# Row sums of a correction for fractional zero points: 32 wide matmuls in place of 128 of one column, in a branch that these inputs jump over

## What is computed

```python
def xattn(x1, x2, x1_scale, x1_zp, x2_scale, x2_zp):   # fake_quant: (clip(round(x/s + z), 0, 255) - z) * s
    return matmul(fake_quant(x1, x1_scale, x1_zp), fake_quant(x2, x2_scale, x2_zp))
def ffn(x, W_base, b_base, W_router, lora_A, lora_B):   # 8 experts of rank 16, the best two per row
    w = normalised top-2 of softmax(x @ W_router.T)
    return x @ W_base.T + b_base + 2 * einsum(lora_B, lora_A @ x, w)
x = x + xattn(layernorm(x), ctx_4096)   # x: 2 x 1024 x 2048, ctx: 2 x 2048 x 2048
x = x + ffn(layernorm(x))
```

## Time and profile before

| | before |
|---|---|
| median of 3 runs | 969.04 us (966.88 to 978.15) |
| the profiled execution | 966.17 us |
| its span, first to last instruction | 964.4 us |
| TensorE busy | 906.4 us (94%) |
| VectorE, ScalarE, GpSimd busy | 610.5 us (63%), 370.9 us (38%), 146.9 us (15%) |
| DMA | 226.59 MB, mean 235 GB/s |

### The profile page before, as it was taken

The page is one execution under the profiler, slowest core; times in us unless marked ns, Lnnn a source line. Parts: engine busy times, 40 slices in busy tenths (PEclk is TensorE's granted clock), DMA queues, the critical chain, the costliest instruction groups (busy, mean ns, idle before and its releaser), DMA issues.

```text
span 964.4 us, 12403 instructions
## 1 busy us (share of the span) xinstructions
PE 906.4 (94%) x4725; PEld 432.5 (45%) x4725; DVE 610.5 (63%) x955; ACT 370.9 (38%) x337; POOL 146.9 (15%) x191
## 2 busy tenths in 40 slices
PE   0599999989999999999999999999999999999997
PEld 0244443434445455454545455444444444444443
DVE  7678578953799875546374546699655365564611
ACT  3867436754265444243324222164213323133100
POOL 2537420332100102010111100010000000000000
PEclk9999999999999999999999999999999999999999
DMA  9998999989874879999999999956479979889621
GB/s 326 346 366 292 327 323 355 305 312 357 254 226 149 226 159 274 166 252 179 241 218 223 192 259 227 364 184 227 146 167 233 228 157 244 210 182 235 150 74 44
DMA packets 269310, 226.59 MB, mean 235 GB/s; under 512 B 221632, under 2 KB 222656, under 8 KB 265280
## 3 DMA queue, kind: packets, MB, share of 16 engines
q1 hardware_dynamic: 258880, 191.15, 74.7%
q0 software_dynamic: 10368, 34.61, 10.7%
HBM read 132.29 MB, written 39.94 MB: 179 GB/s over the span
## 4 chain that ended last, share of the span: by engine, by line
PE 72%; DMA 9%; DVE 8%; issue 6%; SPq 2%; ACT 2%; POOL 1%; POOLq 0%; DVEq 0%; ACTq 0%
PE PS L1645 57%; PE PS L1577 8%; PE PS L1662 4%; PE PS L1680 4%; DMA XR<-x 2%; DMA x1d<-XR 2%; DVE XR L1089 2%; DVE ST L1012 1%; DVE ST L1096 1%; DMA Yb<-x1d 1%; DMA XV<-XU 1%; SPq L533 1%; DMA HT<-HW 1%; DMA XT<-NX 1%; POOL CU L708 1%
## 5 line engine op out<-in xcount | busy, mean ns | idle before, releaser
L1645 PE MATMUL PS<-WS,XT 128*128 128x512 f16 x2736 | 596.3, 379 | 3.5 <-DVE OQ L1343 2.2
L1645 PEld LDWEIGHTS PS<-WS,XT 128*128 128x128 f16 x2736 | 267.1, 98 | 325.9 <-DVE OQ L1343 3.7
L1577 PE MATMUL PS<-QC,QT 128*128 128x512 bf16 x1024 | 227.4, 385 | 46.0 <-ACT QT L781 37.5
L1343 DVE SCALAR_TENSOR_TENSOR OQ<-PS,ZI,OQ 128x512 f32<-128x512 f32 x124 | 90.8, 747 | 157.2 <-PE PS L1662 78.5
L1577 PEld LDWEIGHTS PS<-QC,QT 128*128 128x128 bf16 x1024 | 100.8, 99 | 171.5 <-issue 53.3
L823 ACT ACTIVATE NX<-Yb 128x1024 f16<-128x1024 f32 x52 | 54.9, 1055 | 117.2 <-DMA XT<-NX 61.3
L708 POOL TENSOR_SCALAR CU<-CS,K,S 128x1024 uint8<-128x1024 f32 x64 | 80.9, 1266 | 121.5 <-DMA CS<-ctx 103.7
L727 POOL DMA_DIRECT2D out<-OQ x64 | 34.7, 543 | 409.4 <-DVE OQ L1343 392.0
L1270 DVE TENSOR_TENSOR NX<-Ya,NX 128x1024 f16<-128x1024 f32 x40 | 48.0, 1222 | 75.3 <-ACT NX L823 75.0
L823 ACT ACTIVATE NX<-Ya 128x1024 f16<-128x1024 f32 x40 | 40.9, 1047 | 97.6 <-DMA XT<-NX 93.2
L791 ACT ACTIVATE QC<-CU,K 128x1024 bf16<-128x1024 uint8 x64 | 69.9, 1137 | 12.5 <-POOL CU L708 8.3
(11 more groups left out here) (135 smaller groups left out, 446.6 us busy)
## 6 DMA issues: line engine op xcount, KB each, us to landing
CS<-ctx SPq DMA_DIRECT2D x64, 512.0 KB, 6.0
OQ<-x1d SPq DMA_DIRECT2D x64, 256.0 KB, 4.3
out<-OQ POOLq DMA_DIRECT2D x64, 256.0 KB, 5.9
Ya<-x1d SPq DMA_DIRECT2D x14, 1024.0 KB, 7.0
Yb<-x1d SPq DMA_DIRECT2D x14, 1024.0 KB, 8.0
XR<-x SPq DMA_DIRECT2D x9, 1024.0 KB, 8.4
x1d<-XR SPq DMA_DIRECT2D x16, 512.0 KB, 7.3
FB<-wt SPq DMA_DIRECT2D x8, 1024.0 KB, 9.8
```

The source lines that it names most:

```text
L1343: stt(OQ[ob][:, :], PS[:, bank(i, b), :], ZI[:, half(i), 1:2].bitcast(F32), OQ[ob][:, :], ALU.mult, ALU.add).then_inc(s_rd, 1)
L1577: ins = pe.matmul(PS[:, 2 * (t % 4) + c, :], QT[t][:, kt, :], QC[h][:, kt, c * CH:(c + 1) * CH], start=(kt == 0), stop=(kt == KT - 1))
L1645: ins = pe.matmul(PS[:, bank(i, b), :], XT[SLOT[i, j]][:, xi, kt, :], WS[half(i)][blk][:, :, kt // 2, wi, kt % 2, :], start=(fresh and n = ...
```

## The change

The row sums of QT are taken by multiplying with a matrix of ones. Before, QT was the stationary operand and one column of ones the moving one: 8 tiles x 16 steps = 128 matmuls that give one column each, with the sum of a row in that row's partition. Now ones are stationary and four row tiles at a time are moving (512 columns): 2 x 16 = 32 matmuls, which put the row sums along the free axis, the same in every partition. To get them back into partitions, VectorE multiplies each 128 x 128 block with the identity and reduces it, which adds two instructions for each of the 8 tiles to its body. To make four tiles one operand, the eight tiles QT become slices of one tensor at the same address.

```diff
-        QT = [at(f"QT{t}", [128, KT, 128], BF16, R3 + t * 4 * KB) for t in range(8)]
+        QA = at("QT", [128, 8, KT, 128], BF16, R3)
+        QT = [QA[:, t, :, :] for t in range(8)]
...
                     for t in range(8):
-                        link(ts(CT[:, t, 0:1], PS[:, 4, t:t + 1], k(NSE2), k(KEE), ALU.mult, ALU.add), s_db, n_db)
+
+                        mine = PS[:, 6, 128 * (t % 4):128 * (t % 4) + 128]
+                        link(tt(mine, PS[:, 4 + t // 4, 128 * (t % 4):128 * (t % 4) + 128], ID[:, :], ALU.mult), s_db, n_db)
+                        link(dve.reduce_sum(CT[:, t, 1:2], mine, AX), s_db, n_db)
+                        link(ts(CT[:, t, 0:1], CT[:, t, 1:2], k(NSE2), k(KEE), ALU.mult, ALU.add), s_db, n_db)
...
-                    for t in range(8):
+                    for a in range(2):
                         for kt in range(KT):
-                            ins = pe.matmul(PS[:, 4, t:t + 1], QT[t][:, kt, :], ON[:, 0:1], start=(kt == 0), stop=(kt == KT - 1))
+                            ins = pe.matmul(PS[:, 4 + a, :], ON[:, :], QA[:, 4 * a:4 * a + 4, kt, :], start=(kt == 0), stop=(kt == KT - 1))
```

## The result

| | before | changed |
|---|---|---|
| median, 7 runs of each side by side | 972.83 us (966.88 to 978.15) | 961.36 us (958.79 to 963.30) |
| ratio | | 0.989, 95% interval 0.986 to 0.992 |
| profiled execution, its span | 964.4 us | 957.0 us |

Three later comparisons of the same two kernels gave 0.9936, 0.9930 and 0.9897; the mean of the four is 0.9913, or 8.4 us.

The account below looks back on a forecast made before the run. TensorE, busy 94% of the span, was taken as the bound. WS 3.1 us earlier and +0.8 for the clock gave -2.3 us: 966.7 us from the 969.04 median, range 962.5 to 971.

Parts of the forecast that it names:

- The miss of the jump: TensorE's second branch, 6.28 us, misses because its target lies two code blocks on; after the change it hits at 0.46 us.
- The rival by which the jump still waits: TensorE's second branch stays long through a late fetch or a cause other than blocks; gain 0, 969.0 us, chance 0.1.
- the larger buffer: TensorE's instruction buffer of 2048: both jumps would hit, the 6.28 us come from something else, the change be worth nothing.
- VectorE's jump: VectorE's branch over its longer body: forecast a hit at 0.07 us; rival, a 6.3 us miss, +0.5, 969.5 us, chance 0.03.
- TensorE's own sum: At the second branch the 3.24 us gap and 1.4 us of half clock go; pass (1, 1) ends 4.6 us earlier, at 268.8.
- so the loads move by 216.43 - 213.35 = 3.1 us, and as the DMA engines are then full without a break, so does the landing of the spills: Weight loads after pass (1, 0) and the spills wsum(T1, 0) waits for come 3.1 us earlier, and WS with them.
- 4.6 where TensorE decides: Upper bound for how much earlier the spills land, if TensorE's row tiles set it: 4.6 us, against 3.1 by volume.
- TensorE's wait before the first product grows to 1.16 + 4.6 - 3.1 = 2.7 us: TensorE's wait for WS before the second half's first product grows from 1.16 to 2.7 us, risking the lower clock.
- +0.8 for the half clock: After the wait before the first product, a half-speed stretch could cost 0 to 1.6 us; half was taken, +0.8.
- From 274 us on ... I give the rest nothing: Second half from 274 us on: TensorE has few waits and all feeds move along, so no gain, 0 us.
- The starting point: Base of the forecast: the runs' median of 969.04 us, 2.9 above the profiled execution's 966.2.
- Whole gain: Rival: spills go ahead of other transfers, WS comes 4.6 us earlier, no clock is lost; -4.6, 964.4 us, chance 0.22.

Follow-up runs that it names:

- e4: Changed kernel with TensorE's skipped body long again (192 matmuls, jump over 386 instructions) at the second branch only; ratio to before 0.992, that branch 0.43 us.
- e2: Changed kernel with its 32 new matmuls written four times, so the jump goes over 386 instructions again; ratio to before 1.002, second branch 5.83 us.
- e3: Kernel before with narrow row sums for two of eight tiles only (jump over 194), no other part of the change; ratio 0.994, second branch 0.23 us.
- e6: Kernel before with the signal s_hd raised in front of the jump instead of behind it, so weight loads are issued earlier; ratio to before 1.004.
- e8: Changed kernel with one more SyncE wait ahead of the weight loads, meant to issue them as late as before; ratio to before 0.996.
- g1: Changed kernel plus a third jump over 30 never-run matmuls in pass (1, 1), putting second-half code fetches 7 us later than in before; ratio to before 0.995.
- f1: Changed kernel unaltered, run again beside versions with shifted code; ratio to before 0.993.
- g4: Changed kernel unaltered, run again beside three versions with a third jump; ratio to before 0.990.
- f2: Changed kernel plus a third jump over 62 never-run matmuls in pass (1, 1), putting second-half code against the blocks as in before; ratio to before 0.996.
- g3: Changed kernel plus a third jump over 62 never-run matmuls at (1, 4, 0), putting second-half code fetches as in before; ratio to before 0.997.
- e1: Kernel before unaltered, run and profiled again; ratio 1.001, second branch 5.62 us.
- e7: Kernel before with only the one QT tensor and VectorE's longer body, TensorE's 128 narrow matmuls kept; ratio to before 1.001, second branch 5.24 us.

## Why the prediction was right and wrong

**The miss of the jump: right.** Blocks of 256 instructions, the block at hand and the next, a target two blocks on: e4 is the sharpest test (same length, 0.43 us), e2 and e3 the plainest. The rival by which the jump still waits fell with it, and so did the larger buffer that it drew on. The same jump missed in seven profiles, with 5.06 to 6.28 us. VectorE's jump stayed at 0.07 us; its miss did not happen.

**TensorE's own sum: right.** Gap and half clock went, and pass (1, 1) ended 0.76 us before the first product at 270.10, at 269.3, where 268.8 was forecast.

**The step "so the loads move by 216.43 - 213.35 = 3.1 us, and as the DMA engines are then full without a break, so does the landing of the spills": mis-sized.** The loads did move by 3.1 us, from 3.5 to 0.4 us behind the start of the last matmul of pass (1, 0). The spills moved further. The step took the full DMA engines of the earlier trace rows for a bound by volume. Measured from the last matmul of pass (1, 0), wsum(T1, 0) came 4.6 us earlier on average (28.7 against 33.4), and in the profile of the changed kernel 6.8 (27.2 against 34.0). A full share does not say how much is moved. Two stretches of before inside that full one show it (DMA share and GB/s stand last), with the transposes that were issued in the second (count, median us to landing):

```profile
230.00:234.00 4.00, 4.00 (x20) 1.83 (x19) 2.00 (x3) 4.00 (x3) 0.46 (x1) 1.00 1.02 405
234.00:236.00 2.00, 2.00 (x11) 0.89 (x10) 0.57 (x1) 0.50 (x1) 2.00 (x5) 1.00 1.26 137
```

```profile
XT<-NX SPq DMA_TRANSPOSE x2, 8.7
```

At a share above 1 in both, 405 GB/s were moved in one and 137 in the other, in which two transposes were issued. e6 and e8 speak against the loads alone. Which transfers give way when the row tiles come earlier was not tried. This was the bound that I had written down as "4.6 where TensorE decides", and it was the right one: the term was -4.2 instead of -3.1 (mean reach 57.4 us in ten kernels with a short branch, without e8, against 61.7 in six with a long one, without e6).

**The step "TensorE's wait before the first product grows to 1.16 + 4.6 - 3.1 = 2.7 us" and its +0.8 for the half clock: wrong for most, right for some.** The wait was 0.76 us in six of the ten, 1.8 in g1, and 2.6 to 3.4 in f1, g4 and e4, of which g4 and e4 then ran at half clock. So the price exists, in a minority of executions.

**The step "From 274 us on ... I give the rest nothing": wrong, and the largest.** It is the term that was left out. With the code fetches elsewhere the second half was 4.2 us shorter on average (695.4 against 691.2). That the place of the code brings a gain is shown by f2 and g3, which put the code back and lost 0.3 and 0.8% against the changed kernel beside them (only the intervals of the second pair lie apart); that it works through fetches at moments when the transposes are on the chain is seen for the wait at 136 (1.8 of the 4.2 us) and open for the rest. It was there to be seen in part: all of the second half's code was moved by 384 instructions against the fetches, and the trace of before had a wait of 1.53 us with a fetch 3.7 us ahead of it, but I took the jump to be the only place where code fetches matter. Together: -4.2 - 4.2 = -8.4 us, which is the mean of the four ratios, 0.9913. That it meets to a tenth is luck: the two means are over different groups of kernels. Over the three profiles of before and the four of the changed kernel alone, the mean reach goes from 61.9 to 57.6 and the mean rest from 693.0 to 690.1 us, -7.2 in all, and rest alone spreads by 6 us between executions of one kernel. The first measurement, 0.989, lies at the lucky end of the four.

**The starting point.** The forecast was set against 969.04 us and a profile of 966.2. Before's medians were 968.6 to 972.8 us, and the one beside the first measurement was the highest. The absolute figure, 966.7 against 961.36, misses by 5.3 us, while the gain misses by 9 beside those runs and by 6 on the mean of the four.

**The chances.** "Whole gain" at 0.22 was the nearest case (964.4), and its -4.6 is about what the reach gained, but even that had nothing from the second half. Faster by over 2% did not happen, as forecast.

## What to carry to other kernels

Code that never runs is not free if a branch jumps over it. Here a jump to the same or the next block of 256 instructions took 0.2 to 0.5 us and one to a target two blocks on 5.1 to 6.3 us, of which the sequencer's lead hid some 3. In before its fetch started only 3.9 us after the branch, at 213.9; what the miss would cost with idle DMA engines no run shows. So keep skipped bodies below one block, or place the branch early in its block. When an edit moves the code of an engine, the rest of the program meets its code fetches at other moments; where DMA waits are tight that alone went with 0.3 to 0.8%, so a small gain needs a control that shifts the code and changes nothing else. And engines that are full of DMA work are no proof that volume sets when one transfer lands.

## What the runs showed of the hardware that was not expected

An idle TensorE is not followed by the lower clock each time. Before the first product e4 waited 3.05 us and f1 3.44 us:

```profile
272.73 22.28 PE L1651 MATMUL PS<-WS,XT 128*128 128x512 f16 x96 [3.05 <-DVE WS L1222]
```

```profile
272.54 20.88 PE L1650 MATMUL PS<-WS,XT 128*128 128x512 f16 x96 [3.44 <-DVE WS L1222]
```

The stretches right behind (granted clock third from the end):

```profile
272.70:276.00 3.30, 3.27 (x9) 1.25 (x10) 3.30 (x2) 3.30 (x2) 0.00 (x0) 0.56 0.90 250
```

```profile
272.50:276.00 3.50, 3.46 (x17) 1.61 (x18) 3.50 (x2) 3.50 (x2) 0.00 (x0) 1.00 0.74 243
```

After the longer idle the clock stayed at the full 2.4 GHz, after the shorter one it fell to 1.2. Behind the long branch e1 idled 2.57 us and kept the clock, e7 idled 2.48 us and had 0.50 in the 3.4 us from 216.0. In the changed kernel an idle of 2.00 us (80.6) was followed by the lower clock and one of 2.50 us (172.1, shown above) was not. The rule of the earlier trace rows that I drew between 2.01 and 2.40 us does not hold; a price for the clock is a chance, not a step.

```profile
80.62 20.41 PE L1582 MATMUL PS<-QC,QT 128*128 128x512 bf16 x86 [2.00 <-DVE QT L1082]
```

```profile
81.00:85.00 4.00, 4.00 (x12) 1.51 (x11) 4.00 (x3) 4.00 (x5) 4.00 (x4) 0.57 0.94 304
172.00:176.00 4.00, 3.92 (x19) 1.82 (x20) 4.00 (x8) 4.00 (x4) 3.05 (x3) 1.00 1.09 391
```
